# Layer normalisations on ScalarE with a shift from GpSimd, and the tie factor as a constant of the scaled product

## The reference

```python
def _layernorm(x):                       # before each block, over the last axis
    mu, var = mean(x), mean(square(x - mu))
    return (x - mu) / sqrt(var + 1e-5)   # the state-space block: a second one with gamma, beta

def fp4_quant_dequant(x):                # blocks of 16 values along the features
    scale = maximum(max(abs(xb)) / 6.0, 1e-12)
    xn = xb / scale
    q = GRID[searchsorted(MID, abs(xn))] * sign(xn) * scale

h = dA_t * h + dBu_t                     # the scan, one step per position
y = einsum('bdn,bn->bd', h, C_t)         # sum over 16 states
```

## Time and profile before

| | |
|---|---|
| median of 3 runs | 4327.49 us (4325.34 to 4328.36) |
| profiled execution | 4323.4 us, span of the core 4321.6 us |
| granted TensorE clock, mean | 0.943 |
| PE busy | 3528.9 us (82%) |
| DVE busy | 3215.6 us (74%) |
| ACT busy | 1959.6 us (45%) |
| POOL busy | 1925.1 us (45%) |
| DMA | 649.65 MB, mean 150 GB/s |
| chain that ended last, by engine | PE 46%, DVE 21%, issue 18%, ACT 9%, POOL 5% |

### The profile page before, as it was taken

The page is one execution under the profiler, slowest core; times in us unless marked ns, Lnnn a source line. Parts: engine busy times, 40 slices in busy tenths (PEclk is TensorE's granted clock), DMA queues, the critical chain, the costliest instruction groups (busy, mean ns, idle before and its releaser), DMA issues.

```text
span 4321.6 us, 41545 instructions
## 1 busy us (share of the span) xinstructions
PE 3528.9 (82%) x13488; PEld 1876.9 (43%) x13488; DVE 3215.6 (74%) x4556; ACT 1959.6 (45%) x3692; POOL 1925.1 (45%) x1122
## 2 busy tenths in 40 slices
PE   5885897789978898879987899788988799878657
PEld 5552454245543454434543455434544345434214
DVE  3243778977688867978688776878679787887994
ACT  0343464534645355534645346353555346553441
POOL 0201643536444454445544464444544445443770
PEclk9997999999999899999999999998999999999998
DMA  3002543744436344363435444363453644354780
GB/s 82 1 1 84 183 149 122 250 155 153 147 129 238 123 141 161 132 227 129 157 125 204 158 154 143 125 238 131 139 164 123 235 129 152 127 197 161 253 281 8
DMA packets 203817, 649.65 MB, mean 150 GB/s; under 512 B 34253, under 2 KB 45520, under 8 KB 197456
## 3 DMA queue, kind: packets, MB, share of 16 engines
q1 hardware_dynamic: 203600, 646.98, 44.8%
HBM read 595.52 MB, written 51.38 MB: 150 GB/s over the span
## 4 chain that ended last, share of the span: by engine, by line
PE 46%; DVE 21%; issue 18%; ACT 9%; POOL 5%; SPq 1%; DMA 1%; DVEq 0%; POOLq 0%; ACTq 0%
PE banks L1257 17%; PE banks L1501 9%; DVE banks L864 7%; PE banks L1438 6%; PE banks L1286 5%; PE banks L1262 5%; DVE sb_arena L871 4%; ACT banks L1223 4%; PE banks L1414 3%; POOL sb_arena L991 3%; DVE sb_arena L792 2%; ACT sb_arena L1028 2%; DVE sb_arena L617 2%; SPq L426 1%; ACT sb_arena L1092 1%
## 5 line engine op out<-in xcount | busy, mean ns | idle before, releaser
L991 POOL TENSOR_TENSOR sb_arena<-sb_arena 128x1024 f32<-128x1024 f32 x512 | 1213.2, 2371 | 871.6 <-PE banks L1501 592.6
L864 DVE TENSOR_TENSOR_SCAN banks<-banks,sb_arena 128x512 f32<-128x512 f32 x1024 | 1198.1, 1215 | 181.7 <-ACT banks L1223 135.0
L1501 PE MATMUL banks<-sb_arena,sb_ident 128*128 128x512 f32 x2048 | 1042.4, 637 | 336.9 <-DVE sb_arena L871 268.2
L1223 ACT ACTIVATE banks<-sb_arena,sb_neg_a 128x512 f32<-128x512 f32 x1024 | 665.4, 682 | 1249.9 <-DVE sb_arena L871 1243.8
L1501 PEld LDWEIGHTS banks<-sb_arena,sb_ident 128*128 128x128 f32 x2048 | 384.6, 200 | 821.0 <-DVE sb_arena L871 430.2
L1028 ACT ACTIVATE sb_arena<-banks 128x512 f32<-128x512 f32 (+4 forms) x752 | 381.1, 519 | 636.4 <-PE banks L1262 447.4
L871 DVE TENSOR_TENSOR sb_arena<-banks,sb_arena 128x512 f32<-128x512 f32 x1024 | 651.1, 677 | 0.0
L1262 PE MATMUL banks<-sb_ident,sb_arena 128*128 128x128 f32 (+1 forms) x2082 | 355.7, 295 | 312.9 <-ACT sb_arena L1028 86.1
L1262 PEld LDWEIGHTS banks<-sb_ident,sb_arena 128*128 128x128 f32 (+1 forms) x2082 | 252.1, 149 | 531.4 <-ACT sb_arena L1028 156.6
L737 DVE TENSOR_REDUCE sb_nmax<-banks 128x1 f32<-128x512 f32 (+3 forms) x352 | 223.2, 637 | 285.6 <-PE banks L1441 284.2
L1257 PE MATMUL banks<-sb_w_gu,sb_arena 128*128 128x352 f32 x1024 | 347.1, 487 | 14.0 <-ACT sb_arena L1028 14.0
(11 more groups left out here) (127 smaller groups left out, 4097.3 us busy)
## 6 DMA issues: line engine op xcount, KB each, us to landing
sb_arena<-rows_bc SPq DMA_DIRECT2D x1024, 512.0 KB, 4.4
kept_xc<-sb_arena SPq DMA_DIRECT2D x16, 1024.0 KB, 4.9
kept_z<-sb_arena SPq DMA_DIRECT2D x16, 1024.0 KB, 4.5
sb_arena<-kept_z SPq DMA_DIRECT2D x64, 256.0 KB, 5.0
sb_arena<-kept_xc SPq DMA_DIRECT2D x64, 256.0 KB, 4.6
kept_zs<-sb_arena SPq DMA_DIRECT2D x8, 1024.0 KB, 6.6
sb_arena<-kept_zs SPq DMA_DIRECT2D x8, 1024.0 KB, 9.5
sb_xin<-in_x SPq DMA_DIRECT2D x8, 512.0 KB, 7.4
```

The source lines that it names most:

```text
L864: v.tensor_tensor_scan(factors, factors, products, 0.0, ALU.mult, ALU.add).then_inc(V.sem, V.mark("scan", K, e))
L991: nc.gpsimd.tensor_tensor(dBu[K % SLOTS], u[:, p % 2].unsqueeze(1).to_broadcast([P, 2, T]), rows_b[K % BS], ALU.mult).then_inc(G.sem, G.ma ...
L1223: nc.scalar.activation(psum[:, e], dt[:, (K // NQ) % 2], ACT.Exp, scale=neg_a[:, s, m, 2 * q + e:2 * q + e + 1]).then_inc(A.sem, A.mark("d ...
L1501: mm = pe.matmul(psum[:, YB], ident[:, :], dBu[K % SLOTS][:, e], start=(q == 0 and e == 0), stop=(q == NQ - 1 and e == 1))
```

## The change

The four VectorE operations of a normalisation leave its queue. ScalarE does them as Identity activations, rstd x x + shift, with the scale and the bias as pointers. The shift, -mean x rstd, is a product on 4 columns that GpSimd makes right after each power; VectorE now writes -mean (`less_mean`) at line 605. In the feed-forward all four activations stand at step 1, in the latents at step 0, in the preparation at step 2. The scalings of line 780 become ScalarE's too, as Copy with a pointer scale, at step 4. VectorE's waits for `rstd` in latents and feed-forward go; it waits for ScalarE's `normed_x` ahead of each `amax` of the input. TensorE's waits for normalised tiles and GpSimd's residual addition now look to ScalarE. In the quantisation line 567 goes; the reciprocal is taken of the plain scale, and the product at line 575 becomes a `scalar_tensor_tensor` that multiplies by `TIE` first, which is now 1 - 2^-22 instead of 1 + 2^-22.

```diff
--- before.py
+++ after.py
@@ -55,7 +55,7 @@
 
 LEAST, MOST = -1e-22, 1e25
 
-TIE = 1.0 + 2.0 ** -22
+TIE = 1.0 - 2.0 ** -22
 
 EXP_SET = "natural_log_exp_and_others"
 
@@ -230,7 +230,8 @@
         x, xin = sb("x", [P, TT, C]), sb("xin", [P, TT, C])
         stats = sb("stats", [P, 2, TT, 6])
         moment = sb("moment", [P, 2, 5, TT])
-        mean, var, ve = sb("mean", [P, 2, TT]), sb("var", [P, 2, TT]), sb("ve", [P, 2, TT])
+        less_mean, shift = sb("less_mean", [P, 2, TT]), sb("shift", [P, 2, TT])
+        var, ve = sb("var", [P, 2, TT]), sb("ve", [P, 2, TT])
         rstd, rstd3, ve3 = sb("rstd", [P, 2, TT]), sb("rstd3", [P, TT]), sb("ve3", [P, TT])
         own_rows = sb("own_rows", [P, 4])
         minus_half, minus_one = sb("minus_half", [P, TT]), sb("minus_one", [P, 1])
@@ -563,16 +564,15 @@
             def scales(amax_, s):
                 after(V.n)
                 v.tensor_scalar(s, amax_, 1.0 / 6.0, 1e-12, ALU.mult, ALU.max).then_inc(V.sem, V.mark())
+
+            def inverse(s, r):
                 after(V.n)
-                v.tensor_scalar(amax_, s, TIE, None, ALU.mult).then_inc(V.sem, V.mark())
-
-            def inverse(amax_, r):
-                after(V.n)
-                v.reciprocal(r, amax_).then_inc(V.sem, V.mark())
+                v.reciprocal(r, s).then_inc(V.sem, V.mark())
 
             def scaled(src, r, qn_, n):
                 after(V.n)
-                v.tensor_tensor(by_block(qn_), by_block(src), by_scale(r, n), ALU.mult).then_inc(V.sem, V.mark())
+                v.scalar_tensor_tensor(by_block(qn_), by_block(src), TIE, by_scale(r, n), ALU.mult, ALU.mult
+                                       ).then_inc(V.sem, V.mark())
 
             def exponents(qn_, qm_):
                 after(V.n)
@@ -602,7 +602,7 @@
                                 ).then_inc(V.sem, V.mark())
                 v.tensor_tensor(moment[:, w, 2], stats[:, w, :, 2], stats[:, w, :, 5], ALU.add).then_inc(V.sem, V.mark())
                 after(V.n)
-                v.tensor_scalar(mean[:, w], moment[:, w, 0], 0.5, None, ALU.mult).then_inc(V.sem, V.mark())
+                v.tensor_scalar(less_mean[:, w], moment[:, w, 0], -0.5, None, ALU.mult).then_inc(V.sem, V.mark())
                 v.scalar_tensor_tensor(moment[:, w, 3], moment[:, w, 1], 0.25, moment[:, w, 1], ALU.mult, ALU.mult
                                        ).then_inc(V.sem, V.mark())
 
@@ -612,10 +612,6 @@
                                        ).then_inc(V.sem, V.mark())
                 after(V.n)
                 v.tensor_scalar(ve[:, w], var[:, w], EPS, None, ALU.add).then_inc(V.sem, V.mark("var", *name))
-
-            def normalize(w, src, dst, t, *name):
-                v.tensor_scalar(dst[:, t], src[:, t], mean[:, w, t:t + 1], rstd[:, w, t:t + 1], ALU.subtract, ALU.mult
-                                ).then_inc(V.sem, V.mark(*name))
 
             def merge(c, n):
                 for i in range(MERGE_N):
@@ -654,19 +650,13 @@
                     if i == 0:
                         moments(1)
                         variance(1, b, "ffn", f)
-                    if i in (2, 5):
-                        w = i // 3
-                        if w == 0:
-                            v.wait_ge(G.sem, G.at("rstd", b, "ffn", f))
-                        normalize(1, x, xh, 2 * w)
-                        normalize(1, x, xh, 2 * w + 1)
                     for w, first in ((0, 2), (1, 6)):
                         if i == first:
-                            after(V.n)
+                            v.wait_ge(A.sem, A.at("normed_x", b, f, 2 * w + 1))
                             amax(pair(xh, w), qx_amax[:, w])
                             scales(qx_amax[:, w], qx_s[:, w])
                         if i == first + 1:
-                            inverse(qx_amax[:, w], qx_r[:, w])
+                            inverse(qx_s[:, w], qx_r[:, w])
                             scaled(pair(xh, w), qx_r[:, w], qnx[w], 2 * C)
                             exponents(qnx[w], qmx)
                         if i == first + 2:
@@ -689,7 +679,7 @@
                             amax(hh, q_amax[:, :])
                             scales(q_amax[:, :], q_s[:, :])
                         if d == 7:
-                            inverse(q_amax[:, :], q_r[:, :])
+                            inverse(q_s[:, :], q_r[:, :])
                             scaled(hh, q_r, qn, F)
                         if d == 8:
                             exponents(qn, qm)
@@ -709,10 +699,6 @@
 
             def latents(n):
                 for i in range(LAT_N):
-                    if i == 0:
-                        v.wait_ge(G.sem, G.at("rstd", n, "first"))
-                        for t in range(TT):
-                            normalize(0, xin, xh, t, "normed", n, t)
                     for j, first in enumerate(LAT_AT):
                         w, m = divmod(j, MT)
                         for r, (to, table) in enumerate(((cs, cos), (sn, sin))):
@@ -766,19 +752,13 @@
                     if i == 2:
                         v.wait_ge(G.sem, G.at("rstd", n, "prep"))
                         v.tensor_tensor(ve3[:, :], rstd[:, 1], rstd[:, 1], ALU.mult).then_inc(V.sem, V.mark())
-                        for t in range(TT):
-                            normalize(1, x, xh, t, "normed2", n, t)
                         after(V.n)
                         v.tensor_tensor(ve3[:, :], ve3[:, :], var[:, 1], ALU.mult).then_inc(V.sem, V.mark())
                         after(V.n)
                         v.tensor_scalar(ve3[:, :], ve3[:, :], EPS, None, ALU.add).then_inc(V.sem, V.mark("var3", n))
                     if i == 4:
-                        v.wait_ge(G.sem, G.at("rstd3", n))
                         v.memset(xs[:, :, 0:PAD], 0.0).then_inc(V.sem, V.mark())
                         v.memset(xs[:, :, PAD + T:TP], 0.0).then_inc(V.sem, V.mark("padded", n))
-                        for t in range(TT):
-                            v.tensor_scalar(xq[:, t], xh[:, t], rstd3[:, t:t + 1], None, ALU.mult
-                                            ).then_inc(V.sem, V.mark("normed3", n, t))
                     for s, first in ((0, 11), (1, 17)):
                         if first <= i < first + 6:
                             half, k = divmod(i - first, DC - 1)
@@ -882,16 +862,23 @@
                 g.wait_ge(V.sem, V.at(*name[1:]))
                 nc.gpsimd.tensor_tensor(dst, src, minus_half[:, :], ALU.pow).then_inc(G.sem, G.mark(*name[0]))
 
+            def shifts(w, *name):
+                g.wait_ge(G.sem, G.at("rstd", *name))
+                nc.gpsimd.tensor_tensor(shift[:, w], less_mean[:, w], rstd[:, w], ALU.mult
+                                        ).then_inc(G.sem, G.mark("shift", *name))
+
             def merge(c, n):
                 for i in range(MERGE_N):
                     if i == 6 and n is not None:
                         power(rstd[:, 0], ve[:, 0], ("rstd", n, "first"), "var", n, "first")
+                        shifts(0, n, "first")
                     yield
 
             def ffn(b, f):
                 for i in range(FFN_N):
                     if i == 1:
                         power(rstd[:, 1], ve[:, 1], ("rstd", b, "ffn", f), "var", b, "ffn", f)
+                        shifts(1, b, "ffn", f)
                     for w, first in ((0, 6), (1, 10)):
                         if i == first:
                             g.wait_ge(V.sem, V.at("grid", b, f, "x", w))
@@ -944,9 +931,11 @@
                 for i in range(PREP_N):
                     if i == 1:
                         power(rstd[:, 1], ve[:, 1], ("rstd", n, "prep"), "var", n, "prep")
+                        shifts(1, n, "prep")
                     if i == 3:
                         power(rstd3[:, :], ve3[:, :], ("rstd3", n), "var3", n)
                     if i == 5:
+                        g.wait_ge(A.sem, A.at("normed2", n, TT - 1))
                         nc.gpsimd.tensor_tensor(x[:, :, :], x[:, :, :], xh[:, :, :], ALU.add
                                                 ).then_inc(G.sem, G.mark("residual", n))
                     yield
@@ -1027,8 +1016,16 @@
             def copy(dst, src, *name):
                 nc.scalar.activation(dst, src, ACT.Copy).then_inc(A.sem, A.mark(*name))
 
+            def normalize(w, src, dst, t, *name):
+                nc.scalar.activation(dst[:, t], src[:, t], ACT.Identity, bias=shift[:, w, t:t + 1],
+                                     scale=rstd[:, w, t:t + 1]).then_inc(A.sem, A.mark(*name))
+
             def ffn(b, f):
                 for i in range(FFN_N):
+                    if i == 1:
+                        a.wait_ge(G.sem, G.at("shift", b, "ffn", f))
+                        for t in range(TT):
+                            normalize(1, x, xh, t, "normed_x", b, f, t)
                     for w, first in ((0, 8), (1, 13)):
                         if i == first:
                             a.wait_ge(E.sem, E.at("xqT", b, f, w))
@@ -1055,6 +1052,10 @@
```

(18 more changed lines are left out.)

## The result

The changed kernel takes 4217.99 us (median of 4 runs, 4215.24 to 4222.97) against 4327.34 us for the kernel before in the same series (4325.34 to 4328.36): a ratio of 0.9749, 95% interval 0.9732 to 0.9766, 109 us less. The forecast was 4224, its range 4198 to 4276. The profiled execution took 4215.2 us (span 4213.5).

The account below looks back on a forecast made before the run. No engine was taken as full, the limit changing by stage. Seven laps of 6.4 + 5.0 + 3.0 + 1.4 gave 110.6 us, cut to 100; 4 for set-up and tail made 104 less, about 4224 us, range 4198 to 4276.

Parts of the forecast that it names:

- the latents: Latents, seven laps: transposes no longer wait for stalled normalisations and the sum runs faster, 6.4 us a lap (4.0 to 7.0).
- the preparation: Preparation, seven laps: TensorE starts earlier as normalisations and scalings leave VectorE, 5.0 us a lap (3.0 to 6.0).
- f = 0: Feed-forward between scan and `hc`, seven laps: second pair and stalled factor leave VectorE, 3.0 us a lap (0.5 to 3.6).
- f = 1: Feed-forward where `hc` covers the power, seven laps: savings behind the stalled scale, 1.4 us a lap (0 to 2).
- the 110 asked for: Sign over the whole kernel: VectorE's busy time down by over 110 us.
- scaled product: Quantisation's product with the added immediate: cost taken as 0, at most 5 us over 102 times.
- the clock's share: Latents: without idle time before, the sum's four matmuls take 1.9 instead of 3.6 us, 1.7 us a lap.
- The front's loss: Feed-forward f = 0: VectorE waits for power, shift and two activations instead of doing the pair itself, losing 0.65 us.
- The deduction: Over seven laps: nine tenths of 110.6 taken, 100 us, because earlier starts sometimes meet transfers that are not earlier.
- B: Rival: stalls move to VectorE's next operation with SBUF sources and the clock falls as before; 4268 us, chance 0.20.
- C: Rival: only the work counts, neither stalls nor clock being on the path; 4306 us, chance 0.07.
- D: Rival: ScalarE's activations delay the next units' factors and the scan starves; slower, 4337 us, chance 0.05.

Follow-up runs that it names:

- e2: Kernel before with only the latents' four normalisations moved to ScalarE: 4282.63 us, ratio 0.9902.
- e3: Kernel before with only the preparation's normalisations and scalings moved to ScalarE: 4283.25 us, ratio 0.9903.
- e7: Kernel before with 18 products by zero on TensorE ahead of its wait for the latents' normalisations: 4307.60 us, ratio 0.9961.
- e10: Kernel before with 26 products by zero on TensorE ahead of its wait for the preparation's scalings: 4320.68 us, ratio 0.9990.
- e9: Changed kernel with five fills of products by zero: two in preparation gaps, one at each feed-forward's front, one ahead of the first `w_x` product: 4193.24 us, ratio 0.9696.
- e1: Kernel before with only the tie factor's part of the change: 4303.17 us, ratio 0.9950.
- e4: Kernel before with only the two feed-forwards' normalisations moved to ScalarE: 4322.07 us, ratio 0.9992.
- e5: Changed kernel with VectorE repeating eight moved operations unused, reading SBUF, TensorE waiting for both engines: 4280.24 us, ratio 0.9898.
- e6: Changed kernel with VectorE repeating eight moved operations unused, reading PSUM, TensorE waiting for both engines: 4228.11 us, ratio 0.9779.
- e8: Changed kernel with fills of 12 and 10 products by zero on TensorE in two gaps of the preparation: 4202.72 us, ratio 0.9719.

## Why the prediction was right

**The bound.** Read by units, the time comes from the four named places: over the seven laps the latents give 46.3 us, the preparation 40.6, f = 0 19.3 and f = 1 9.4 (its seventh time is in the eighth lap), where 44.8, 35.0, 21.0 and 9.8 were forecast. The waits are those that the forecast named: TensorE's 4.60 us are gone, and its 6.64 are 1.39. VectorE's busy time fell by 161.5 us, over the 110 asked for.

**Prices.** Normalisation 0.61 forecast, 0.59 measured; four in a row 2.1, measured 2.06 to 2.07; scaling 0.51, measured 0.50 with 1.70 for four; shift 0.2, measured 0.20; scaled product 0, measured 0.001. The Trainium skill's estimate for a normalisation, 585 ns by its page "ScalarE: Activation LUTs", was as good, but its rule against the move would have cost the gain: the moved operations are dearer by 0.2 us each and the kernel is 85 us faster for moving them in two stages (runs e2 and e3).

**Latents.** 6.4 forecast, 4.33 + 2.58 measured at the place (2.5 in most laps). The forecast's own terms, 4.9 for the sum's start and 1.7 for the clock, add up to 6.6 and not 6.4. Run e7 confirms the clock's share, which I had at 1.7 from the sum alone; I had left out the transposes, 1.97 us for 1.04. Over the whole kernel it was 43.0 (run e2) for 7 x 6.4 less 0.9 of the set-up, 43.9. That it comes so close is in part luck: the place gives more than forecast, and 1.65 a lap, which was not forecast, goes in the attention.

**Preparation.** The term that was mis-sized: 5.0 forecast, 6.24 measured between units 48 and 50, and 42.4 us (35 to 49) in run e3 for 37. The activations were where the sum had them, and so was the wait (5.25 us less): counted from the first scan of unit 48, TensorE's transposes start 5.17 us earlier. What the step lacked is that the transposes behind a gap of 6.64 us run at the low clock (0.50 granted from 1793 to 1797 us), and behind the shorter one at the full clock (1.00 from 1745.5 to 1748.5). From their start to the scan of unit 50 it is 2.83 us instead of 3.90, 1.07 less, and 5.17 + 1.07 is 6.24. Run e10 confirms the 1.07, since its fill alone shortens the way to the end of the copies by as much; there most of it is covered by VectorE until unit 50, so that it is worth the whole 1.07 only once VectorE's stall is gone too. I counted this in the latents and not here. It didn't show in the total because up to 1.96 is given back at unit 54, again by the clock (run e9).

**f = 0 and f = 1.** 3.0 forecast, 2.75 measured in the lap of the table; 1.4 forecast, 1.1 measured at units 5 and 6 and 0.23 more at unit 9, 1.34 in all. The front's loss is 2.53 us of waiting instead of 1.13 and 0.74 for the pair, 0.66, as forecast (0.65). The tie factor is nearly all of the gain in f = 0 (run e1, 2.53 a lap at one unit); the move of the normalisations gives little (run e4, 3.5 us for both). The scale in f = 1 did grow (1.48 to 1.90) and, as worked out ahead, at no cost, since it ends with the same product.

**The deduction.** Nine tenths of 110.6 were 100; the laps gave 104.2. The size is right by luck. The four places gave some 5 us more than forecast and the rest of the laps lost 10: 7.9 at unit 54 and 5.0 at unit 21, with 2.9 won elsewhere. Both losses go with the low clock (run e9, and the granted clocks at unit 21). The reason I gave, transfers that an earlier start meets, is not what the runs show. GpSimd's waits for spread rows did grow, from 170.8 to 190.3 us, but VectorE's scans wait no longer for GpSimd's products than before. Their group, before and then after (the idle time ahead of them, and what ended it):

```profile
L864 DVE TENSOR_TENSOR_SCAN banks<-banks,sb_arena 128x512 f32<-128x512 f32 x1024 | 1198.1, 1215 | 181.7 <-ACT banks L1223 135.0 <-POOL sb_arena L991 46.4 <-issue 0.3
```

```profile
L844 DVE TENSOR_TENSOR_SCAN banks<-banks,sb_arena 128x512 f32<-128x512 f32 x1024 | 1197.9, 1215 | 212.3 <-ACT banks L1234 163.2 <-POOL sb_arena L980 47.0 <-POOL sb_arena L956 1.0
```

**The rivals.** B falls by run e1 (the scale's mean unchanged) and by units 12 and 42, where the next operation reads PSUM and doesn't stall. In the whole change the scale did gain 140 ns on each of 32 x tiles, 4.4 us of busy time, and lost as much on the h tiles; line 792 stayed as it was (1007 and 1001 ns). C falls by runs e5 and e6: the same work costs 62 us or 10 depending on where it reads. D's wait exists, 4.06 us of VectorE before the scans of unit 50, but in time that was a stall before. In the feed-forwards, where run e4 has it alone, it cost nothing measurable.

## What to carry to other kernels

An engine's busy time has stalls in it: look for operations of one kind whose longest time is several times their median, see what the other engine began just before them, and price them by what they hold up. Such an operation can be removed, moved to an engine that isn't disturbed (none of ScalarE's 128 normalisations takes over 601 ns, their median being 585 to 589), or, as shown here for a `tensor_scalar`, given its source in PSUM. And look up the granted clock behind each idle gap of TensorE that you close or open, in every stage and not only where the gap is largest. A gap that can't be closed is worth filling with products by zero, as long as the fill is shorter than the gap and something is waiting for what stands behind it: the same kind of fill was worth 16.9 us in the latents (run e7), 4.6 in the preparation (run e10), and nothing ahead of a sum that nobody waited for (the first fill of run e8).

## What I had not expected of the hardware

A `tensor_scalar` on 128x256 that reads PSUM beside a running GpSimd product takes 0.55 us at most, its usual time; the same from SBUF takes up to 2.5 us, and the choice is worth 52 us in the pair of runs above. It is slower where nothing disturbs it (535 against 390 to 418 ns), so it pays only where the stall is.

Eighteen products by zero that nobody uses, 0.21 us each, made the kernel before 16.9 us faster by holding TensorE's granted clock at 1.00 instead of 0.60 over the next 7 us.
